# Moving every second full-width second-pair square of batches 0 and 1 from ScalarE to VectorE

## The reference, cut to what matters

```python
q = (h @ Wq) / 4;  k = h @ Wk;  v = h @ Wv          # 16 heads of 16 features
inter_o = phi(q) @ S;  inter_z = phi(q) @ z         # phi(x) = outer(x, x)
A = einsum(q, k) ** 2 * mask                        # lower triangle
o = (inter_o + A @ v) / (inter_z + A.sum(-1) + 1e-5)
S, z = S + phi(k).T @ v, z + phi(k).sum()
```

## Time and profile before

| | us |
|---|---|
| median of 3 runs | 904.36 (899.43 to 904.51) |
| the profiled execution | 906.11 |
| its span | 904.4 |

### The profile page before, as it was taken

How to read it: one execution, slowest core, us unless ns; L and a number is a source line. 1 busy time by engine, 2 the same in 40 slices (tenths; PEclk the granted TensorE clock), 3 DMA queues, 4 the chain that set the end, 5 groups by cost and what they waited for, 6 DMA issues and landing times.

```text
span 904.4 us, 12060 instructions
## 1 busy us (share of the span) xinstructions
PE 777.9 (86%) x3927; PEld 381.4 (42%) x3927; DVE 493.9 (55%) x1913; ACT 448.0 (50%) x678; POOL 158.0 (17%) x340
## 2 busy tenths in 40 slices
PE   4898987789899978979989988868899950999998
PEld 3353323234333334323334322444386640658667
DVE  5636553541546123597998894266779886430000
ACT  1246775776667655768776777422412200241220
POOL 2221232221221111212332212011013000200100
PEclk9898987899999998979999999788899985899999
DMA  4481532210323221213431223000110013000001
GB/s 147 166 244 58 187 117 71 70 52 20 117 64 146 78 59 27 64 51 118 150 105 48 75 63 59 1 8 2 40 40 32 16 34 74 13 0 24 24 0 47
DMA packets 53146, 61.29 MB, mean 68 GB/s; under 512 B 21391, under 2 KB 32323, under 8 KB 53083
## 3 DMA queue, kind: packets, MB, share of 16 engines
q1 hardware_dynamic: 51995, 56.32, 20.6%
q0 software_dynamic: 1088, 4.19, 1.5%
HBM read 37.17 MB, written 23.32 MB: 67 GB/s over the span
## 4 chain that ended last, share of the span: by engine, by line
PE 62%; DVE 19%; ACT 7%; DMA 4%; issue 4%; SPq 2%; POOL 0%; ACTq 0%; DVEq 0%
PE psO L1299 13%; PE psS L1282 13%; PE psS L1446 9%; PE psW L1456 8%; PE psW L1351 5%; PE psW L1374 3%; ACT ARENA L866 3%; DVE FOLD L1072 3%; PE psW L1342 2%; DVE STATS L1127 2%; PE psW L1358 2%; PE psW L1383 2%; PE psW L1436 2%; SPq L613 2%; DVE FOLD L1012 2%
## 5 line engine op out<-in xcount | busy, mean ns | idle before, releaser
L866 ACT ACTIVATE ARENA<-psS 128x1024 f32<-128x1024 f32 (+3 forms) x384 | 300.7, 811 | 113.4 <-PE psS L1282 110.4
L1282 PE MATMUL psS<-ARENA 96*128 96x512 bf16 (+3 forms) x768 | 197.3, 348 | 29.1 <-ACT ARENA L866 28.1
L780 POOL TENSOR_SCALAR_AFFINE_SELECT ARENA<-ARENA 128x256 f32<-128x256 f32 x256 | 111.2, 438 | 417.3 <-ACT ARENA L866 415.1
L1299 PE MATMUL psO<-ARENA 128*32 128x512 f32 (+3 forms) x1536 | 173.1, 524 | 2.7 <-ACT ARENA L871 2.5
L1282 PEld LDWEIGHTS psS<-ARENA 96*128 96x128 bf16 x768 | 57.1, 100 | 218.6 <-ACT ARENA L866 124.5
L1456 PE MATMUL psW<-W2E,ARENA 128*128 128x256 f32 x512 | 111.8, 379 | 0.7 <-ACT ARENA L887 0.4
L1456 PEld LDWEIGHTS psW<-W2E,ARENA 128*128 128x128 f32 x512 | 96.7, 189 | 16.4 <-issue 1.4
L940 ACT ACTIVATE ARENA<-psS,BEFF 128x512 f32<-128x512 f32 x64 | 43.4, 687 | 89.7 <-PE psS L1446 89.7
L1174 DVE TENSOR_TENSOR X<-X,psW 128x512 f32<-128x512 f32 x32 | 21.9, 688 | 97.1 <-PE psW L1374 52.2
L1351 PE MATMUL psW<-XX,ARENA 128*128 128x512 f32 x128 | 67.6, 635 | 5.0 <-DVE ARENA L1162 3.0
L1446 PE MATMUL psS<-XX,MIXA 128*128 128x512 f32 x128 | 58.4, 611 | 3.4 <-ACT ARENA L940 2.7
(11 more groups left out here) (145 smaller groups left out, 814.5 us busy)
## 6 DMA issues: line engine op xcount, KB each, us to landing
ARENA<-qk_parts SPq DMA_DIRECT2D x192, 128.0 KB, 2.7
qk_parts<-ARENA SPq DMA_DIRECT2D x16, 768.0 KB, 3.5
out<-ARENA SPq DMA_DIRECT2D x16, 256.0 KB, 2.1
X<-in_x POOLq DMA_DIRECT2D x3, 1024.0 KB, 7.3
dist<-ARENA SPq DMA_DIRECT2D x1, 2560.0 KB, 8.2
MORE<-dist SPq DMA_DIRECT2D x16, 160.0 KB, 2.2
path<-MORE SPq DMA_DIRECT2D x16, 80.0 KB, 2.0
path<-FOLD SPq DMA_DIRECT2D x16, 80.0 KB, 2.1
```

Source lines behind the costliest of these rows:

```text
L780: pool.affine_select(out=blk, in_=blk, compare_op=ALU.is_ge, fill=0.0, base=0, pattern=[[0, 2], [1, P]], channel_multiplier=-1).then_inc(s ...
L866: nc.scalar.activation(A[:, (2 * G + a) % A_PAIRS, :, 0:N], psS[:, a, :, 0:N], ACT.Square).then_inc(s_sq, 1)
L1282: ins = nc.tensor.matmul(psS[:, a, j, 0:N], KST[0:STACK, g % 2, 2 * a + j, kt * P:(kt + 1) * P], QST[0:STACK, g % 2, 2 * a + j, q0:q0 + N] ...
L1299: ins = nc.tensor.matmul(psO[32 * j:32 * j + 32, o % 2, q0 - qc * HALF:q0 - qc * HALF + N], V1[:, kt, GH * g + j], A[:, (2 * G + j // 2) % ...
```

## The change

For 32 pairs, VectorE does what ScalarE did. `by_vector` lists them: batches 0 and 1, pair a = 1, full width, even step number, which are steps 0, 4, 6 and 8 of every 12. ScalarE skips these. VectorE, at the place of the `scores` unit in the common list, waits for the scores and for the slot of `A`, copies the pair from PSUM to its slot, waits for that copy, and multiplies the slot by itself in place. It counts `s_sq_vec` after the product. Everyone who waited for `s_sq` now asks `squared(pair)` for the semaphore and the count: the mask on GpSimd, the scores of the next step, and the products, which wait for their two pairs separately. The plan itself and its sizes are not changed.

```diff
+    by_vector = [2 * (b * NS + n) + 1 for b in range(2) for n in range(NS) if span(n)[1] == HALF and n % 2 == 0]
+
+    def squared(pair):
+
+        if pair in by_vector:
+            return s_sq_vec, by_vector.index(pair) + 1
+        return s_sq, pair + 1 - sum(1 for p in by_vector if p < pair)
...
+        s_sq_vec = sem("s_sq_vec")
...
             def mask(b, n, a):
 
                 pair = 2 * (b * NS + n) + a
-                pool.wait_ge(s_sq, pair + 1)
+                pool.wait_ge(*squared(pair))
...
                     G = b * NS + n
+                    if 2 * G + a in by_vector:
+                        continue
                     act.wait_ge(s_qk, 2 * G + a + 1)
...
+                elif kind == "scores":
+                    _, b, n, a = u
+                    nth = 2 * (b * NS + n) + a
+                    if nth in by_vector:
+                        N = span(n)[1]
+                        dve.wait_ge(s_qk, nth + 1)
+                        if nth >= A_PAIRS:
+                            dve.wait_ge(s_av, (nth - A_PAIRS) // 2 + 1)
+                        raw = A[:, nth % A_PAIRS, :, 0:N]
+                        vec(nc.vector.tensor_copy(raw, psS[:, a, :, 0:N]))
+                        settled()
+                        nc.vector.tensor_tensor(out=raw, in0=raw, in1=raw, op=ALU.mult).then_inc(s_sq_vec, 1)
...
                 if G:
-                    pe.wait_ge(s_sq, 2 * G + a - 1)
+                    pe.wait_ge(*squared(2 * G + a - 2))
...
-                pe.wait_ge(s_sq, 2 * G + 2)
+                for a in range(2):
+                    pe.wait_ge(*squared(2 * G + a))
```

## The result

Median of four runs after: 938.57 us (937.37 to 939.21), against 902.16 for the kernel before in the same comparison (899.43 to 904.51, four runs). Ratio 1.040, interval 1.036 to 1.044: slower by 36.4 us. The forecast was 937. The profiled execution took 937.37, its span 935.6, so its difference to the one before is 31.2.

What follows compares the result with a forecast made beforehand. It took TensorE's in-order queue as the bound, with little lost to ScalarE. 27.6 - 2.8 - 3.5 + 10.0 + 1.5 = 32.8; 906.1 + 32.8 - 1.75 = 937 us, own range 930 to 945 (55%), wider range 918 to 953.

Steps and rivals of the forecast that it cites:

- Price of a square: One moved square on VectorE: copy 1.23 plus product 1.23, 2.5 us with the wait, 1.5 more than on ScalarE.
- Lateness at the slot: psS slots released late to the next step's scores: 22 us by slack at 32 places, plus 5.5 for busy VectorE, 27.6.
- Pushes: Work queued on VectorE behind the two new instructions starts later and holds up TensorE at uncovered places: +10.0 us.
- Given back by ScalarE: Relieved ScalarE returns time in batches 0 and 1: -2.8 us at 123 to 198 us, -3.5 at 198 to 337.
- clock: TensorE's clock in batches 0 and 1: no term in the sum; a lower clock was only a rival, at 15%.
- rival D: New gaps lower TensorE's clock in batches 0 and 1 from 0.93 to 0.88, 12 us more: 949; 15%; sign: under 0.90.
- Port sharing: VectorE's SBUF products stretched beside GpSimd masks: 0.1 us each at 16 masked steps, +1.5 us.
- Stretches: Signs to look for: a shift of 4.5 us in 92 to 123 us, and of 5 in 230 to 246.
- A: ScalarE was the bound; TensorE's waits for its squares go, at most 13.2 us: 891, faster; 2%.
- B: The lateness falls into TensorE's 31.5 us of idle time in the changed stretch: 900 to 912; 6%.
- C: Slots late, but VectorE's pushes absorbed by later waits and all 13.2 us of ScalarE waits returned: 919, up to 926; 22%.
- E: The change doesn't do what it says, in skipped pairs or semaphore counts: excluded as far as seen.

Runs made afterwards that it cites:

- e1: Changed kernel, but the slot of psS is released after VectorE's copy, not after the product: 926.56 us, ratio 1.027 to the kernel before.
- e6: Changed kernel with only the eight pairs on VectorE where a push was predicted uncovered, slot released after the product: 922.45 us, ratio 1.024 to the kernel before.
- e7: Changed kernel with only the eight pairs of predicted uncovered pushes on VectorE, slot released after the copy: 924.59 us, ratio 1.025 to the kernel before.
- e4: Changed kernel, but the eight pairs where a push was predicted uncovered go back to ScalarE, 24 stay on VectorE: 920.52 us, ratio 1.019 to the kernel before.
- e9: Changed kernel with only five pairs of batch 0 on VectorE, where ScalarE also mixes weights, slot released after the copy: 903.83 us, ratio 1.001 to the kernel before.
- e3: Changed kernel, but all squares on ScalarE; VectorE waits for the same scores, then runs two unread reductions of equal length: 927.75 us, ratio 1.028 to the kernel before.
- e5: Changed kernel with slot release after the copy and the eight pairs of predicted uncovered pushes back on ScalarE: 909.04 us, ratio 1.009 to the kernel before.

## Why the prediction was right, and which terms were off

The direction, the size and the mechanism hold: TensorE's queue stands still for VectorE, which is in order and waits itself. By its terms:

- **Price of a square**, 2.5: measured 2.48. Both lengths came from the slope between 256 and 512 columns and held to 0.01 us. The slope was taken between a product and a copy, so it took both for equally fast, without a row that said so; 1.220 and 1.224 bear it out.
- **Lateness at the slot**, 27.6. In after, the steps of the shift that fall at S(n+1,1) behind a moved pair sum to 26.6: mostly 0.8 to 1.7 each, 3.61 once, none at seven places. By slack: 8.1 at the six places without any (8.7 in the sum), 11.9 at the ten typical ones (10.0), 5.4 at the nine with 1.05 to 1.4 (3.2), 1.2 at the seven with plenty (0). The 5.5 for a VectorE that isn't free belong on top of the numbers in brackets.
- **Pushes**, +10.0. In after the eight places cost 2.6 at step 4 of batch 0, 3.5 at steps 6 and 8, 2.0 at step 32, and in batch 1 6.5 at steps 12 and 16, 3.8 at step 32 and 1.9 at step 44: 20.4, of which 6.7 are slots already in the 26.6 (0.69, 0.81, 1.10, 3.61, 0.46). That leaves 13.7 for the pushes, 3.7 more than forecast. Part of them went over ScalarE, a way that the prediction names at steps 12 and 16 only: at step 8 of batch 0 the 1.27 of S(9,0), shown above.
- **Given back by ScalarE**, -2.8 and -3.5, and **clock**, 0: 26.6 + 13.7 = 40.3 is 0.7 more than the 39.6, so what came back and what the clock took nearly cancel. TensorE's waits for ScalarE fell only 2.7 in all (13.2 to 10.5), where I had 6.3 of both kinds; part of what ScalarE gave back was taken again by its waits for VectorE. The clock I had only as rival D: it fell from 0.93 to 0.89 and TensorE's busy time grew by 9.0; how much of that is added time isn't shown. **This net term, -6.3 where it came out at -0.7, is the one that was mis-sized most;** the pushes come next. They hardly show in the medians, since these stand 3 us under the 39.6.
- **What failed as a cause** is not in the sum but in how I read it. I took slots (27.6) and pushes (10) as two separate losses, of which each could be cured alone, and so expected e1 near +13. It kept +24. At the eight places the early release gave nothing that the runs can tell (e6 and e7), so they keep their 18 to 22 us; some 4 us of clock and 4.4 us of waits for the mask stand in e1's trace besides, and no run splits the miss between the three. Seen by place instead, the sum holds: 18.2 at 24 places with e4, 22.5 at eight with e6.
- **Port sharing**, +1.5: nothing. The product took 1.224 in every one of 32 places. More on this below.
- **Stretches**, of which the prediction names two: 4.5 in 92 to 123 us, measured 3.94; 5 in 230 to 246 us, measured 6.5, the excess at steps 12 and 16. The first scores of batch 2, forecast near 370, start near 373.

So the sum is 32.8 against 36.4 by the medians and 39.6 in the changed stretch. That the 937 lies within 2 us of 938.57 is in part luck: it started at 904.36, the median of the runs shown, and not at 902.16, from which the same sum gives 935.

**The rivals.** A (ScalarE the bound) falls: the kernel got slower with 32 squares less on ScalarE, which still waits 58.8 us for scores, and e9's five bought nothing. B (hidden) falls: 3.94 us were lost where TensorE had no idle time. C (pushes absorbed) falls by e3 and e7, which lose 25 us each, the one with no slot late by VectorE and the other with the slots released early. D came in part: 0.89, just under the 0.90 that I named as its sign. The Trainium skill, "TensorE: Matmul & The Clock Gate", A second HAM failure mode, describes idle gaps between groups of matmuls as making the clock swing between its two levels. This case's traces agree in this much: the stretch at 97 to 132 us, with 3.7 us idle of 35, kept 1.00, and the one with gaps had 0.84 before and 0.81 with more of them. They don't show what decides where a spell falls: 160 to 180 us ran at 1.00 after and at 0.74 in e1, and from step 36 to step 40 of batch 0 the clock was 1.00 before, though TensorE idled for 3.3 of 9.3 us.

E falls: ScalarE has 64 squares where it had 96, and VectorE the 32.

**Open.** How much of the clock's 9.0 us lies on the path: no run holds the clock still. What of e3's 25 us is VectorE alone and what is ScalarE's fuller queue. And how the 9 us that e5 keeps divide between the clock, the mask and the rest: its shift is 3.5 after batch 0, falls to 1.2 by step 32 of batch 1 and rises by 4.0 behind it.

## What to carry to other kernels

An instruction that waits for another engine holds its own engine for the wait as well as for its length, and everything behind it in the queue starts later. What that costs depends on what stands there: the same wait with a hold of 1.22 us cost 4. Before moving work to an engine "with room" list, for each place, what stands behind it and who waits for that: here giving back eight places of 32 took away half of the loss, and the busy share (61%) showed nothing of it. A delay can also go over a third engine. Delays that end at the same stretch of a queue overlap, so a cure for one may be worth nothing until the other is cured, and trying each alone and both shows it. And a slack measured in the trace of before acts like a threshold: a hold of 1.22 us cost 4 us, one of 2.48 cost 36.

## What the runs showed of the hardware that was not expected

One product of the 32 ran beside a mask of GpSimd, at 87.45 us in the profile after (start, length, engine, line, instruction; the second row is two masks), and the masks' group of the page:

```profile
87.45 1.22 DVE L1190 TENSOR_TENSOR ARENA<-ARENA 128x1024 f32<-128x1024 f32 x1
...
87.50 1.79 POOL L789 TENSOR_SCALAR_AFFINE_SELECT ARENA<-ARENA 128x256 f32<-128x256 f32 x2 [22.18 <-ACT ARENA L877]
```

```profile
L789 POOL TENSOR_SCALAR_AFFINE_SELECT ARENA<-ARENA 128x256 f32<-128x256 f32 x256 | 111.9, 443 | 451.2 <-ACT ARENA L877 413.1
```

VectorE's two-input instruction wasn't stretched, 1.224 as ever; the mask was held, two of them in 1.79 where one takes 0.44 in the mean, so about 0.9 us longer, to near the product's end. The splits of line 1178 show both orders in this profile: one that began at 287.12, 0.07 us behind a mask, took 0.875 and the mask 0.41; one that began at 130.03, 0.33 us ahead of a mask, took 0.69 and the mask 0.62. The Trainium skill, "SBUF — State Buffer", Who interferes with whom, says that issue order decides which of the two blocks. The trace agrees in all three. I had priced it on VectorE, from the longest of the earlier trace rows, as if the mask always came first. It cost nothing: the other products met no mask, and TensorE's waits show none for GpSimd there.

The clock's slow spells move from execution to execution even in stretches that are the same: 30 to 57 us ran at 0.87 before and at 1.00 after, 550 to 580 at 0.81 before and 0.94 after; with 580 to 610 us it is 8.4 us together. In a comparison of two single traces that is a quarter of this change's effect, and only the medians tell it apart.
